# Attention score tiles in rounds of four over four row groups, and score pairs in the second attention

## What is computed

```
block 0:  h = LN(x)*(1+sc)+sh;   x += g * (windowed self-attention, 8 windows of 128, rolled by 64)   attention 1
          h = LN(x)*(1+sc)+sh;   x += g * (cross-attention to 154 context tokens, top 16 scores only)   attention 2
          x += g * swiglu(LN(x)...)                          hidden size 1024
block 1:  x += softmax(q k^T / 4) v, 1024 x 1024, + t        attention 3
          x += masked cross-attention to 154 tokens + t      attention 4
          x += gelu(LN(x) w1) w2 + t
```

## Time and profile before

| | us |
|---|---|
| median of 3 runs | 2396.81 (2392.38 to 2397.28) |
| the profiled execution | 2378.54 |
| its span, first to last instruction | 2376.8 |
| TensorE busy | 2245.9 (94%) |
| DVE busy | 916.9 (39%) |
| ACT busy | 784.5 (33%) |
| mean granted TensorE clock | 0.761 of 2.4 GHz |

### The profile page before, as it was taken

How to read it: one execution, slowest core, us unless ns; L and a number is a source line. 1 busy time by engine, 2 the same in 40 slices (tenths; PEclk the granted TensorE clock), 3 DMA queues, 4 the chain that set the end, 5 groups by cost and what they waited for, 6 DMA issues and landing times.

```text
span 2376.8 us, 25891 instructions
## 1 busy us (share of the span) xinstructions
PE 2245.9 (94%) x9132; PEld 1091.3 (46%) x9132; DVE 916.9 (39%) x2815; ACT 784.5 (33%) x1626; POOL 258.2 (11%) x504
## 2 busy tenths in 40 slices
PE   6999989999898999999999999999999998999998
PEld 4577866656465343343333333333323323555356
DVE  3322328768786653333233222243222212333021
ACT  2222226665656222422233222133222235233221
POOL 0010014434443100000010000010000000001020
PEclk9876767689999898996588555587555568798799
DMA  3010110000000000010000000000000000000000
GB/s 121 11 48 18 38 34 10 6 1 4 1 19 1 23 1 1 1 45 0 1 1 1 0 0 1 0 1 7 0 0 1 1 1 1 1 8 2 6 16 18
DMA packets 22096, 26.78 MB, mean 11 GB/s; under 512 B 4204, under 2 KB 19634, under 8 KB 21708
## 3 DMA queue, kind: packets, MB, share of 16 engines
q1 hardware_dynamic: 21059, 25.03, 3.3%
q10 hardware_dynamic: 909, 0.10, 0.0%
HBM read 21.58 MB, written 3.08 MB: 10 GB/s over the span
## 4 chain that ended last, share of the span: by engine, by line
PE 87%; DVE 4%; ACT 4%; issue 3%; POOL 1%; DMA 1%; another core or an unknown queue 0%; SPq 0%; ACTq 0%; DVEq 0%; POOLq 0%
PE bank L785 17%; PE bank L822 16%; PE bank L862 8%; PE bank L747 7%; PE bank L726 5%; PE bank L762 5%; PE bank L777 3%; PE bank L818 3%; PE bank L705 3%; PE bank L797 3%; PE bank L882 3%; PE bank L832 2%; PE bank L684 2%; PE bank L712 1%; PE bank L732 1%
## 5 line engine op out<-in xcount | busy, mean ns | idle before, releaser
L1042 ACT ACTIVATE pr<-bank 128x512 f32<-128x512 f32 x656 | 377.9, 597 | 1192.5 <-PE bank L822 779.6
L1255 DVE TENSOR_REDUCE part_max<-bank 128x1 f32<-128x512 f32 x512 | 330.3, 686 | 769.2 <-PE bank L785 769.1
L785 PE MATMUL bank<-slot 32*128 32x512 f32 x1024 | 477.7, 852 | 2.1 <-DVE part_max L1255 1.4
L822 PE MATMUL bank<-slot 32*128 32x512 f32 x1024 | 422.3, 899 | 0.0
L785 PEld LDWEIGHTS bank<-slot 32*128 32x128 f32 x1024 | 174.6, 258 | 251.1 <-issue 196.5
L822 PEld LDWEIGHTS bank<-slot 32*128 32x128 f32 x1024 | 109.5, 249 | 260.0 <-issue 184.1
L862 PE MATMUL bank<-pr,v 128*17 128x512 f32 x1024 | 195.1, 845 | 8.0 <-ACT pr L1042 8.0
L1305 POOL TENSOR_SCALAR var_eps<-mean_var 128x4 f32<-128x4 f32 x24 | 5.5, 227 | 1727.6 <-DVE mean_var L1219 1727.4
L747 PE MATMUL bank<-h_t,w_m 128*128 128x512 f32 x256 | 136.3, 658 | 6.5 <-ACT h_t L984 3.1
L882 PE MATMUL bank<-kc,slot 32*128 32x154 f32 x512 | 117.1, 354 | 4.6 <-ACT exp_all L1059 3.8
L1252 DVE TENSOR_REDUCE neg_max<-bank 128x4 f32<-128x512 f32 x64 | 44.0, 691 | 174.2 <-PE bank L777 173.7
(11 more groups left out here) (147 smaller groups left out, 2501.5 us busy)
## 6 DMA issues: line engine op xcount, KB each, us to landing
w_m<-in_L_xcond_w_m SPq DMA_DIRECT2D x1, 2048.0 KB, 8.0
w_m<-in_L_xcond_w_m SPq DMA_DIRECT2D x2, 1024.0 KB, 6.9
w<-in_L_xcond_w SPq DMA_DIRECT2D x2, 1024.0 KB, 6.5
w_ada<-in_L_xcond_w_ada SPq DMA_DIRECT2D x1, 1792.0 KB, 10.5
x_sb<-in_x SPq DMA_DIRECT2D x6, 256.0 KB, 6.8
res_row<-rows_dram SPq DMA_DIRECT2D x12, 128.0 KB, 3.3
out_x<-x_sb SPq DMA_DIRECT2D x6, 256.0 KB, 2.1
wa<-in_L_xcond_w_qkv SPq DMA_DIRECT2D x1, 768.0 KB, 7.8
```

Source lines behind the costliest of these rows:

```text
L785: last = nc.tensor.matmul(bank[:, :], q[rows, t * P:(t + 1) * P], k[rows, kc * 512:(kc + 1) * 512], start=True, stop=True)
L822: last = nc.tensor.matmul(bank[:, :], k[rows, kt * P:(kt + 1) * P], q[rows, qc * 512:(qc + 1) * 512], start=True, stop=True)
L1042: nc.scalar.activation(m.pr[:, u % NPR, :], g.bank("s", gi, i)[:, :], ACT.Exp).then_inc(g.free("s", gi, i), 1)
L1255: nc.vector.tensor_reduce(m.part_max[:, slot, h * TB + i // 8, i // 4 % 2:i // 4 % 2 + 1], bank[:, :], axis=AX.X, op=ALU.max).then_inc(don ...
```

## The change

`group_run` is written anew. An attention runs in rounds: 4 per group in attention 1, 32 in attention 3, 6 in attention 4. A round holds two s tiles of one group and two m tiles of the next, which leads by 2, 4 or 2 rounds, and the four tiles have four different row groups (in attention 4 the m tiles are put in another order for that, and two of six rounds have one full-array s tile with the m pair). The four tiles get their banks as before, but TensorE runs them in one step, `scores`: first product 0 of every tile, then product 1 of every tile, and so on; the wait for a tile's bank stands at its own first product. The weighted sum `pv` follows one round after the round of its last s tile.

Banks: m and s tiles have 3 to 6, and 1 to 6 in groups 20 to 23 (before: 2 to 6 in all of attention 3). In exchange `o_turn` and the token work of stage (5, 0) have bank 0 alone in groups 19 to 23, and the stages (3, 1), (4, 1) and the turns of groups 16 to 18 have 0 to 2.

In attention 2 the two `c_score` tiles of a query tile become one step, `c_scores`: both waits first, then their four products, alternating between two row groups; it stands 1.15 steps ahead of the first tile's selection instead of 1.6 ahead of each.

The plan times of the token work and loads around the attentions are shifted to match. Arithmetic, buffers, transfers and the work of DVE, ACT and POOL are the same.

```diff
+ROUNDS = {1: 4, 3: 32, 4: 6}
+LEAD = {1: 2, 3: 4, 4: 2}
+M_HEADS_4 = ((0, 2), (0, 3), (0, 0), (0, 1), (1, 2), (1, 3), (2, 2), (2, 3), (1, 0), (1, 1), (2, 0), (2, 1))
+def s_tiles(a, x):
+    if a != 4:
+        return [2 * x, 2 * x + 1]
+    return [x // 3 * 5 + i for i in ((0,), (1, 2), (3, 4))[x % 3]]
@@ banks_of
-        return (2, 3, 4, 5, 6) if attention(step[1]) == 3 else (3, 4, 5, 6)
+        return (1, 2, 3, 4, 5, 6) if 20 <= step[1] < 24 else (3, 4, 5, 6)
...
-        return (0, 1) if attention(step[1]) in (2, 3) else (0, 1, 2)
+        return (0, 1) if attention(step[1]) == 2 else (0,) if 19 <= step[1] < 24 else (0, 1, 2)
...
-    return (0, 1) if (s, b) in ((2, 1), (3, 0), (3, 1), (4, 0), (4, 1), (5, 0)) else (0, 1, 2)
+    return (0, 1) if (s, b) in ((2, 1), (3, 0), (4, 0)) else (0,) if (s, b) == (5, 0) else (0, 1, 2)
@@ group_run
+    for c in range(-lead, 9 * rounds):
+        t, width = time(c), time(c + 1) - time(c)
+        gs, xs = c // rounds - 1, c % rounds
+        gm, xm = (c + lead) // rounds, (c + lead) % rounds
+        gi_s, gi_m = (a - 1) * 8 + gs, (a - 1) * 8 + gm
+        weighed = [("s", gi_s, i) for i in s_tiles(a, xs)] if gs >= 0 else []
+        maxima = [("m", gi_m, i) for i in (2 * xm, 2 * xm + 1)] if gm < 8 else []
+        tiles = [x for both in zip(weighed, maxima) for x in both] if len(weighed) == len(maxima) else maxima + weighed
+        plan.at(t, *tiles, ("scores", *tiles))
+        plan.at(t + 0.3 * width, *[("m_red",) + x[1:] for x in maxima], *[("exp",) + x[1:] for x in weighed])
+        if gm < 8 and xm == rounds - 1:
+            plan.at(t + 0.9 * width, *([("m_neg", gi_m)] if a == 3 else []), ("m_turn", gi_m), ("m_copy", gi_m), ("max_rows", gi_m))
+        if gs >= 0 and xs % per == per - 1:
+            d = xs // per
+            t1, width = time(c + 1), time(c + 2) - time(c + 1)
+            plan.at(t1 + 0.4 * width, ("pv", gi_s, d))
...
@@ topk_run
+                    plan.at(start + (v - 1.15) * step, ("c_score", gi, t, 0), ("c_score", gi, t, 1), ("c_scores", gi, t))
                     for hf in range(2):
                         t0 = start + v * step
-                        plan.at(t0 - 1.6 * step, ("c_score", gi, t, hf))
@@ make_plan (the rounds' planned widths; token work and loads are shifted with them)
-    W = 13.0
+    R = 3.2
+    W = ROUNDS[1] * R
...
-    plan.spread(token_slots(2, 0), T + 5.4 * W, T + 8.6 * W)
+    plan.spread(token_slots(2, 0), T + 6.0 * W, T + 9.4 * W)
...
-    W = 56.0
+    R0, R1 = 2.6, 1.75
@@ tensor_program
-        if step in plan.bank:
+        if step in plan.bank and kind not in ("m", "s", "c_score"):
...
+        elif kind == "scores":
+            tiles = step[1:]
+            for j in range(4):
+                for tile in tiles:
+                    if j == 0:
+                        for signal in g.emptied(*tile):
+                            since(pe, signal)
...
+                    if j < parts_of(tile):
+                        into, left, right = operands(m, tile, j)
+                        last = nc.tensor.matmul(g.bank(*tile)[:, into], left, right, start=True, stop=True)
+                        if j == parts_of(tile) - 1:
+                            last.then_inc(m.m_mm if tile[0] == "m" else m.s_mm, 1)
...
+        elif kind == "c_scores":
+            _, gi, t = step
+            b, u = batch_of(gi), half_heads(gi)[0]
+            for hf in range(2):
+                for signal in g.emptied("c_score", gi, t, hf):
+                    since(pe, signal)
...
+            for hh in range(2):
+                for hf in range(2):
+                    r = 2 * (gi % 2) + hf
...
```

More of the change, by code:

```diff
@@ L232, in token_slots, with group_run, time @@
     return out
[L235 to L258, removed]
+def group_run(plan, a, start, first, then):
+    rounds, lead = ROUNDS[a], LEAD[a]
+    per = rounds // PV_STEPS[a]
+    turn = 5 * rounds
+    def time(c):
+        return start + first * (min(c, turn) + lead) + then * max(c - turn, 0)
+    for c in range(-lead, 9 * rounds):
[14 more added lines that the diff above has]
+            plan.at(t1 + 0.4 * width, ("pv", gi_s, d))
+            if (d + 1) % (PV_STEPS[a] // 2) == 0:
+                half = (d + 1) // (PV_STEPS[a] // 2) - 1
+                plan.at(t1 + 0.9 * width, ("o_copy", gi_s, half))
+                plan.at(t1 + 1.5 * width, ("o_turn", gi_s, half))
+                plan.at(t1 + 1.9 * width, ("o_norm", gi_s, half))
+    return time(9 * rounds)
@@ L310, in make_plan @@
     plan.spread(ctx, T + 3.3 * W, T + 5.2 * W)
-    plan.spread(token_slots(2, 0), T + 5.4 * W, T + 8.6 * W)
+    plan.spread(token_slots(2, 0), T + 6.0 * W, T + 9.4 * W)
     step = 2.6
-    A2 = end + 2
+    A2 = end + 3
     half = 32 * step
@@ L764, in tensor_program @@
                 last.then_inc(m.p_mm, 1)
[L765 to L784, removed]
-                last = nc.tensor.matmul(bank[:, :], q[rows, t * P:(t + 1) * P], k[rows, kc * 512:(kc + 1) * 512], start=True, stop=True)
-            else:
-                h = (i + 2) % 4
-                u, odd = half_heads(gi)
-                if i == 0:
-                    for n in range(2):
-                        for signal in g.projected(gi, n, (0,)):
-                            pe.wait_ge(*signal)
-                    if gi == 24:
-                        pe.wait_ge(m.kc_in, 16 * 5)
-                rows = slice(HW * h, HW * h + HW)
-                for j, t in enumerate(range(i // 4 * 3, min(i // 4 * 3 + 3, TB))):
-                    last = nc.tensor.matmul(bank[:, j * S2:(j + 1) * S2], q[rows, t * P:(t + 1) * P], m.kc[rows, u, odd, b, :], start=True, stop=True)
-            last.then_inc(m.m_mm, 1)
@@ new lines, in tensor_program @@
+        elif kind == "scores":
[5 more added lines that the diff above has]
+                            since(pe, signal)
+                        at, gi, i = attention(tile[1]), tile[1], tile[2]
+                        if tile[0] == "s":
+                            if i == 0:
+                                order = plan.n("max_rows", gi)
+                                pe.wait_ge(m.max_in[order % 2], 16 * (order // 2 + 1))
+                                if gi == 24:
+                                    pe.wait_ge(m.tails_done, 8)
+                        elif at == 1 and i % 4 == 0:
+                            for signal in g.projected(gi, i // 4, (0, 1)):
+                                pe.wait_ge(*signal)
+                        elif at != 1 and i == 0:
+                            for n in range(2):
+                                for signal in g.projected(gi, n, (0, 1) if at == 3 else (0,)):
+                                    pe.wait_ge(*signal)
+                            if gi == 24:
+                                pe.wait_ge(m.kc_in, 16 * 5)
+                    if j < parts_of(tile):
[3 more added lines that the diff above has]
+                            last.then_inc(m.m_mm if tile[0] == "m" else m.s_mm, 1)
@@ L878, in tensor_program @@
                         pe.wait_ge(*g.freed("ck", mt))
-            r = 2 * (gi % 2) + hf
-            rows = slice(HW * r, HW * r + HW)
             for hh in range(2):
-                last = nc.tensor.matmul(bank[:, hh * C:hh * C + S2], m.q2[b][rows, u, t * P:(t + 1) * P], m.kc[rows, u, hh, b, :], start=True, stop=True)
-            last.then_inc(m.c_mm, 1)
+                for hf in range(2):
+                    r = 2 * (gi % 2) + hf
+                    rows = slice(HW * r, HW * r + HW)
+                    last = nc.tensor.matmul(g.bank("c_score", gi, t, hf)[:, hh * C:hh * C + S2], m.q2[b][rows, u, t * P:(t + 1) * P],
+                                            m.kc[rows, u, hh, b, :], start=True, stop=True)
+                    if hh == 1:
+                        last.then_inc(m.c_mm, 1)
         elif kind == "c_tail":
```

105 lines of the change are left out of this document (57 added, 48 removed).

## The result

The changed kernel takes 1713.04 us (median of 3 runs, 1712.03 to 1724.65), 0.717 of the time before (95% interval 0.713 to 0.721). Its profiled execution took 1712.03 us with a span of 1710.2.

A forecast was written before the change was run, and what follows sets the result against it. TensorE bounds it, by its clock and how many 32-row products run at once. Terms -285, -5, -290, -105, -15, -65 sum to -765 of 2376.8; +40 for clock, then 0.8% to the median: 1665 us, range 1540 to 1890.

The forecast's parts named there:

- Rival A: The forecast itself: rounds four wide and clock near 2.4 GHz; 1540 to 1780 us; chance 0.70.
- B: Rounds four wide, but TensorE stays at 1.2 GHz wherever attention is alone; 1945 us; chance 0.13.
- D: s and m tiles do not run side by side, each with its wait serialises; 2700 us; chance 0.03.
- C: All stages: full clock, but waits at TensorE's queue head cost a reading time per round; 1880 us; chance 0.13.
- the signs: Group 19 steps 4.4 us, group 21 3.5; PEclk above 0.9, attentions 1 to 4; DVE near 75% in attention 3.
- Lone groups: Attention 3 groups 19, 21 and 22, without token work: 475 us now, 190 after; -285 us.
- Token work of attention 3: Attention 3 beside token work, 776 to 1317 and 1482 to 1641: 700 us to 410, -290 us (-200 to -330).
- Attention 1: Short-product tiles in four-wide rounds save 144; bank waits, joints and token chains give some back: -105 us (-50 to -140).
- Attention 2: A pair of score tiles goes out together but waits for both its banks: -15 us, from -40 to +15.
- Attention 4: Score products, 146 us busy, become 48 rounds of 46 us, less bank waits and joints: -65 us (-30 to -90).
- group 23: Attention 3, s tiles only: 60 us now at 0.94 of the clock, 55 after; -5 us.
- Clock dips: Stretches that TensorE bounds run at 0.94 to 0.95 clock, not 1.00: 3% of roughly 1250 us, +40 us.

The follow-up runs named there:

- Either fix alone: Kernel before with only the new m-tile heads: 1927.73 us, ratio 0.806; or changed kernel with m tiles in its s tiles' two row groups: 1979.05 us.

## Why the prediction was right where it was, and wrong where it was not

The time, 1713, lies 48 us over the 1665 forecast and inside the range. Rival A happened: full clock and four-wide rounds. B and D did not: no lone group is under 1.00, and eight records of four row groups take 1.13 to 1.14 us. C priced a lone step at 5.3 us; here it is 3.98 to 4.58. The kernel with all waits first did have C's step with four banks (5.22) but not with six (4.10), and lost 65 us, not the 215 between the two forecasts. Of the signs, clock above 0.9 held but for attention 2 (0.82) and the maxima alone (0.86), and DVE's share in lone groups was 59 to 66%, not 75.

**Lone groups.** The steps were priced at 4.4 us (group 19, four banks) and 3.4 to 3.5 (groups 21, 22, six banks); groups 19 and 22 have 3.98. A step with four banks, in group 17, takes 4.58. Group 19 has six banks for its m tiles, since these belong to group 20: a misreading of `banks_of`. With six banks, I let every tile of the second round find a free bank. The trace has two start at 1304.52, 0.96 us after the round of 1303.56; the other two wait for their bank's reader and start at 1305.36 and 1305.50, after the exp and the maximum that began at 1304.71 and 1304.76. Groups 19 and 22 together took 128 us, predicted 127 plus joints: two errors that cancel.

**Token work of attention 3.** Here the 94 us are lost (-486 for -580). First, the step that failed is the subtraction: 1095 us of busy time, "the lone groups and group 23 hold 533 of it, so 562 fall here and about 138 are token work". The rows of L785 and L822 overlap each other in time, so their sum is more than TensorE's time in them; the earlier trace rows show it, for in those four stretches TensorE was busy 524 us in all, less than 533. Laid over each other record by record, token work and transpositions kept TensorE busy 191 us before in these stretches, and keep it busy 175 now (649 to 1049 and 1114 to 1284 us), not 125: +50. Second, attention 3's own score products and sums take 58 to 63 us in each group, with token work or without (62 in group 19), and 40 in the maxima alone, so token work fills little of the bank waits; in all 348 us where 319 were forecast: +29. Third, TensorE is idle 59 us there where I allowed about 24, for the token work's own chains lie bare: +35 (timeline at 776 us, idle in brackets):

```profile
778.69 1.97 PE L779 MATMUL bank<-ident,x_hat 128*128 128x128 f32 x8 [1.38 <-DVE x_sb L1282]
780.59 1.75 PE L857 MATMUL bank<-slot 32*128 32x512 f32 x8
782.27 1.05 PE L895 MATMUL bank<-pr,v 128*17 128x512 f32 x8
785.04 1.95 PE L814 MATMUL bank<-h_t,w_m 128*128 128x512 f32 x4 [1.72 <-ACT h_t L1023]
```

About 12 us of overlap between own and token products comes off. That is 50 + 29 + 35 - 12 = 102 for the stretches outside groups 19, 22 and 23, where 468 us were forecast (410, and 58 for group 21 with its joint) and 570 measured. The work of stage (5, 0) also lies in groups 20 and 21, not in 20 alone, so group 21 took 90 us where I had priced it as lone.

**Attention 1** saved 134 for 105, near the end of its range. The condition that I had set, short products side by side as long ones, held only because of the order product by product: without it the saving was 80.

**Attention 2** had the wrong sign, inside its range (+15): TensorE's saving there is real and worth nothing: it is busy 336 us with pairs and 388 with single tiles, and the stage takes 437 and 431. DVE is busy 322 us in both; that its chain with ACT and POOL sets the length is the likely reading, but no run shortened that chain.

**Attention 4** saved 59 for 65, **group 23** 5 for 5. **Clock dips** were put at +40 on top: the TensorE-bound stretches ran at 0.94 to 1.00, the first maxima alone at 0.86, and what that costs is already in the stage lengths; so this term hid 40 of the 94 us above. (The prediction's "0.82 to 0.84" beside token work leaves out 1482 to 1641 us, 0.71 in the earlier trace rows.) The 0.8% from profiled run to median (12 us) hid another part; here it is 0.06%.

**Place of the waits.** I wrote that all waits first "would be much the same, since the last bank decides". It was said of four banks, and there it fails (5.22 for 4.58); it holds only for the step with six (4.10 for 3.98). For the kernel it is 65 us wrong, 28 of them in attention 3 and 29 in attention 4, at a lower clock.

**Four products side by side.** Four 32-row products ran as fast as two (1.14 us, 766.22, against 1.13 in the earlier trace rows), and the next round can start 0.96 us after (1303.56 to 1304.52), not 1.25. So the speedup of 3.07 in the Trainium skill (TensorE: Matmul & The Clock Gate, section "Measured speedup vs the span model"), which stood behind 1.25, did not show:

```profile
766.22 1.14 PE L857 MATMUL bank<-slot 32*128 32x512 f32 x8
```

## What to carry to other kernels

Give neighbours in TensorE's queue different row groups, and where a tile has several short products, interleave them product by product; put each wait at the first product that needs it. Read the granted clock beside the busy share: a TensorE that is 100% busy at 0.50 can be faster with the same work; here a denser order, and even added full-array products, gave time back. Busy times of lines that overlap must not be added up to find what is left for others.

## What was not expected of the hardware

The clock answers one and the same step in two ways within one execution: 6.94 and 13.29 us with the added products, and with rounds two wide 4.79 us for twelve steps on end (one of them longer by a transposition) and about 10.11 for ten, some 200 us apart. Adding 96 full-array products made three groups 105 us shorter. Either fix alone recovers 413 to 464 of 684 us. Which property of the work the clock follows (rows in use, products side by side, or both) stays open: no run changed one of them alone.

And products of different row groups need not start in the order of the queue: in the earlier trace rows the plan has s and m tiles in turn, yet three s tiles start from 1307.41 and the m tiles queued between them from 1309.28. The Trainium skill (TensorE: Matmul & The Clock Gate, section "The mechanism") describes products as starting strictly in order; this trace differs.
